# A graph network on one core: addition and residual placed after the next block's weighing, and the projection of q, k and v one block later, ahead of the feed-forward

## The reference

```python
for l in range(2):                                     # layers 0 and 1
    xn = layernorm(h, ln1_g[l], ln1_b[l])
    q, k, v = (xn @ w[l] + b[l] for w, b in (q, k, v))  # 8 heads of 32
    scores = einsum('ehd,ehd->eh', q[dst], k[src]) * scale
    attn = segment_softmax(scores, dst)                # with a self edge per node
    agg = segment_sum(attn * v[src], dst)              # 0 for a node without edges
    h = h + agg @ wo[l] + bo[l]
    xn2 = layernorm(h, ln2_g[l], ln2_b[l])
    h = h + gelu(xn2 @ w1[l] + b1[l]) @ w2[l] + b2[l]
x = x + h
...
mod_k = K[src] + 0.2 * rel_w[edge_type]                # layer 2, 4 heads of 64
out = softmax-weighted sum of V[src]  @ Wo + bo
x = x + layernorm(out + node_features) * gamma + beta
```

## Time and profile before

| | |
|---|---|
| median of 3 runs | 5655.94 us (5652.53 to 5657.53) |
| the profiled execution | 5652.02 us, of it the span 5650.4 us |
| busy: PE, DVE | 3852.2 us (68%), 3863.6 us (68%) |
| busy: POOL, ACT | 3129.7 us (55%), 1896.3 us (34%) |
| DVE waits for `feed_out` (L1252, L1256 on L1570) | 227.2 us in 48 waits, 215.8 us in 48 |
| DVE waits for the exponentials (L1167 on L1361) | 212.3 us in 130 waits |
| DVE waits for the square roots (L578 on L574) | 163.6 us in 192 waits |

### The profile page before, as it was taken

The page is one execution under the profiler, slowest core; times in us unless marked ns, Lnnn a source line. Parts: engine busy times, 40 slices in busy tenths (PEclk is TensorE's granted clock), DMA queues, the critical chain, the costliest instruction groups (busy, mean ns, idle before and its releaser), DMA issues. The chain is left out here.

```text
span 5650.4 us, 101635 instructions
## 1 busy us (share of the span) xinstructions
PE 3852.2 (68%) x17126; PEld 2788.6 (49%) x17127; DVE 3863.6 (68%) x6685; ACT 1896.3 (34%) x4023; POOL 3129.7 (55%) x3068
## 2 busy tenths in 40 slices
PE   2057664688887877746878778777746666666665
PEld 2023332466665665534656656555534455455444
DVE  9633333787776666637877766666469989888876
ACT  5023331233333333322333343333422333333333
POOL 0422224777666655426777655554267777666643
PEclk9987776788888988877989888888866766766666
DMA  4022224676666555436666665554256665555542
GB/s 180 7 62 93 94 94 123 188 216 205 191 184 189 172 166 155 136 106 187 212 213 195 190 192 171 162 162 146 81 145 180 184 178 167 163 163 154 144 131 84
DMA packets 361805, 870.95 MB, mean 154 GB/s; under 512 B 142032, under 2 KB 154813, under 8 KB 361748
## 3 DMA queue, kind: packets, MB, share of 16 engines
q0 software_dynamic: 243088, 718.69, 43.2%
q1 hardware_dynamic: 111604, 119.56, 6.8%
q10 hardware_dynamic: 7056, 32.12, 1.4%
HBM read 791.89 MB, written 149.65 MB: 167 GB/s over the span
## 5 line engine op out<-in xcount | busy, mean ns | idle before, releaser
L1039 POOL DMA_INDIRECT kv<-kv_dram,idx x2616 | 2699.7, 1032 | 1598.8 <-issue 751.2
L1506 PE MATMUL ps_acc<-kv,ident 128*128 x5232 | 1499.1, 457 | 328.9 <-DVE kv L1179 327.7
L1506 PEld LDWEIGHTS ps_acc<-kv,ident 128*128 128x128 f32 x5232 | 1218.6, 236 | 635.2 <-issue 412.1
L1101 DVE TENSOR_TENSOR kv<-kv,ps_q 128x1024 f32 x654 | 785.0, 1213 | 177.1 <-issue 103.7
L1106 DVE TENSOR_REDUCE sc<-kv 128x32 f32 (+2 forms) x654 | 785.5, 1211 | 17.5 <-DVE kv L1101 13.1
L1179 DVE TENSOR_TENSOR kv<-kv,ps_q x654 | 753.6, 1216 | 20.7 <-issue 8.2
L1500 PE MATMUL ps_acc<-acc_scaled,ident 128*128 128x256 f32 x306 | 149.2, 581 | 567.1 <-DVE zrun L1171 567.1
L1557 PE MATMUL ps_big<-xnaT,w_ffn 128*128 128x128 f32 x3136 | 389.4, 284 | 142.5 <-ACT xnaT L1407 142.5
L1557 PEld LDWEIGHTS ps_big<-xnaT,w_ffn 128*128 128x128 f32 x3136 | 372.1, 198 | 164.4 <-ACT xnaT L1407 83.0
L1407 ACT ACTIVATE xnaT<-ps_t,ln 128x128 f32<-128x128 f32 x196 | 79.0, 453 | 1068.5 <-PE ps_t L585 898.7
L1500 PEld LDWEIGHTS ps_acc<-acc_scaled,ident 128*128 128x128 f32 x306 | 61.5, 251 | 620.6 <-DVE zrun L1171 620.6
(11 more groups left out here) (206 smaller groups left out, 5024.8 us busy)
## 6 DMA issues: line engine op xcount, KB each, us to landing
rec_in<-rec_dram SPq DMA_DIRECT2D x147, 512.0 KB, 5.1
rec_dram<-rec_out POOLq DMA_DIRECT2D x98, 512.0 KB, 3.4
kv<-kv_dram,idx POOLq DMA_INDIRECT x2616, 3.7
rec_dram<-rec_in ACTq DMA_DIRECT2D x49, 640.0 KB, 3.0
windows<-kv SPq DMA_DIRECT2D x46, 408.0 KB, 2.6
rec_in<-rec_dram SPq DMA_DIRECT2D x49, 128.0 KB
w_ffn<-in_L_gnn_w SPq DMA_DIRECT2D x4, 1024.0 KB, 6.4
meta<-slot_meta SPq DMA_DIRECT2D x153, 24.0 KB, 2.6
```

The costliest lines, as they stand in the source:

```text
L1039: pool.indirect_dma_start(kv[:, u * W + slot, :], None, kv_dram[l], bass.IndirectOffsetOnAxis(ap=idx[:, u, slot:slot + 1], axis=0), bounds ...
L1101: nc.vector.tensor_tensor(at, at, q, ALU.mult).then_inc(s["mul"], 1)
L1506: mm = nc.tensor.matmul(ps_acc[:, 0:D], ident[:], at[:, :, slot, :].rearrange("p a d -> p (a d)"), start=False, stop=False, skip_group_che ...
```

## The change

Four things are done at once.

1. On DVE `second(b-2)` and `residual(b-1)` stand behind `weigh` of block b, at the end of the iteration. `maxima`, `rescale`, `weight_sums` and `weigh` follow each other without them. This holds in layer 2 too.
2. The scales that go with them are taken one iteration later, right behind `start`: `scales1(b-2)` and `scales2(b-3)`. On ACT the first normalisation stands before the second.
3. q, k and v of the next layer are projected for block b-4 instead of b-3 (`DEPTH` 4), on PE before the feed-forward, and q goes into the second half of the bank of `ps_t`, so that PE waits for ACT's copies of that bank. ACT's `record(b-4)` follows the copy of the first transposes.
4. `feed_out` is cut in two halves, with `project_sums` between them.

```diff
--- before.py
+++ after.py
@@ -46,7 +46,7 @@
 HEADS = [8, 8, 4]
 RING = 4
 SETTLED = []
-DEPTH = 3
+DEPTH = 4
 SCATTER_LAG = 5
 STORE_LAG = 5
 
@@ -207,7 +207,8 @@
         eps_col = sb("eps_col", [P, 1])
 
 
-        ps_t = pb("ps_t", [P, 512])[:, 0:D].rearrange("p (c n) -> p c n", c=KD)
+        ps_t_q = pb("ps_t_q", [P, 512])
+        ps_t = ps_t_q[:, 0:D].rearrange("p (c n) -> p c n", c=KD)
         ps_t2_w = pb("ps_t2_w", [P, 512])
         ps_t2 = ps_t2_w[:, 0:D].rearrange("p (c n) -> p c n", c=KD)
         ps_w = pb("ps_w", [P, 512])
@@ -923,13 +924,13 @@
                 last, chunks_before, earlier, rounds_before = counts
                 return (round_number(rounds_before + earlier), chunks_before + earlier * CPS, last)
 
-            def iterate(eng, iteration, peeled=DEPTH, whole=NB - 1 if typed else NB):
+            def iterate(eng, iteration, peeled=2 if typed else DEPTH, whole=NB - 1 if typed else NB):
 
                 for b in range(peeled):
                     iteration(b)
                 with eng.Fori(peeled, whole) as b:
                     iteration(b)
-                for b in range(whole, NB + DEPTH):
+                for b in range(whole, NB + peeled):
                     iteration(b)
 
             def last_block(b):
@@ -1271,10 +1272,16 @@
                         def second_part():
                             if exists(b - 2):
                                 second(b - 2)
+                        def earlier_scales():
+                            if exists(b - 2):
+                                scales1(b - 2)
+                            if exists(b - 3) and not typed:
+                                scales2(b - 3)
                         if exists(b):
                             counts = blocks.next(b)
                             k, chunk0, filled = last_round(counts)
                             start(b)
+                            earlier_scales()
 
                             def finish_last():
                                 if exists(b - 1):
@@ -1304,23 +1311,17 @@
                                 with dve.If(earlier == 0):
                                     finish_last()
                             scores(b, k, chunk0, filled, finish_late if late else lambda: None)
-                            second_part()
                             maxima(last, k, chunk0, filled)
+                            rescale(last, b, k)
+                            weight_sums(b, k)
+                            weigh(k, chunk0, filled)
                         else:
+                            earlier_scales()
                             if exists(b - 1):
                                 finish(b - 1, dve.snap(blocks.rounds, min_val=1))
-                            second_part()
+                        second_part()
                         if exists(b - 1):
                             residual(b - 1)
-                        if exists(b):
-                            rescale(last, b, k)
-                        if exists(b - 2) and not typed:
-                            scales2(b - 2)
-                        if exists(b - 1):
-                            scales1(b - 1)
-                        if exists(b):
-                            weight_sums(b, k)
-                            weigh(k, chunk0, filled)
 
                     extras = dve.alloc_register(f"l{l}_extras")
                     dve.reg_mov(extras, 0)
@@ -1447,11 +1448,13 @@
                         to = rec_out[:, one(b % OUT_RING), :]
                         act.wait_ge(s["qkv"], b + 1)
                         nc.scalar.copy(flat(to[:, :, 0:2 * D]), ps_kv)
-                        nc.scalar.copy(flat(to[:, :, 2 * D:3 * D]), ps_w[:, 0:D]).then_inc(s["recq"], 1)
+                        nc.scalar.copy(flat(to[:, :, 2 * D:3 * D]), ps_t_q[:, D:2 * D]).then_inc(s["recq"], 1)
 
                     def iteration(b):
                         if exists(b - 2) and not typed:
                             feed_forward(b - 2)
+                        if exists(b - 4) and not typed:
+                            record(b - 4)
                         if exists(b - 3) and not typed:
                             turn_normed(b - 3)
                         if exists(b - 2) and not typed:
@@ -1478,12 +1481,10 @@
                         if exists(b - 1):
                             act.wait_ge(s["var1"], b)
                             deviation(0, s["sd1"])
+                        if exists(b - 1):
+                            normed1(b - 1)
                         if exists(b - 2) and not typed:
                             normed2(b - 2)
-                        if exists(b - 1):
-                            normed1(b - 1)
-                        if exists(b - 3) and not typed:
-                            record(b - 3)
                         if exists(b):
                             free_unused(k, filled)
 
@@ -1559,16 +1560,15 @@
                             if f % 4 == 3:
                                 mm.then_inc(s["f1"], 1)
 
-                    def feed_out(b):
+                    def feed_out(b, half):
                         to = ps_w[:, D:2 * D]
-                        if not isinstance(b, int) or b >= 2:
-                            pe.wait_ge(s["recq"], b - 1)
-                            settle(pe)
-                        bias(to, B_2 + l * D)
-                        for f in range(KF):
+                        if half == 0:
+                            bias(to, B_2 + l * D)
+                        for f in range(half * KF // 2, (half + 1) * KF // 2):
                             pe.wait_ge(s["g"], b * KF + f + 1)
                             mm = nc.tensor.matmul(to, gT[:, f, :], w_2[:, f, :], start=False, stop=(f == KF - 1))
-                        mm.then_inc(s["f2"], 1)
+                        if half == 1:
+                            mm.then_inc(s["f2"], 1)
 
                     def turn_normed(b):
                         pe.wait_ge(s["xn2"], b + 1)
@@ -1582,29 +1582,35 @@
                         project_kv(l + 1, xnbT)
 
                     def next_q(b):
-                        if not isinstance(b, int) or b + 1 < NB:
-                            pe.wait_ge(s["second"], 2 * b + 3)
+                        if not isinstance(b, int) or b + 2 < NB:
+                            pe.wait_ge(s["xTs1"], b + 3)
                             settle(pe)
-                        project_q(ps_w[:, 0:D], l + 1, xnbT).then_inc(s["qkv"], 1)
+                        project_q(ps_t_q[:, D:2 * D], l + 1, xnbT).then_inc(s["qkv"], 1)
 
                     def iteration(b):
                         if exists(b - 2) and not typed:
                             turn_hidden(b - 2)
                         if exists(b - 3) and not typed:
                             turn_normed(b - 3)
+                        if exists(b - 4) and not typed:
+                            next_kv(b - 4)
+                            next_q(b - 4)
                         if exists(b - 2) and not typed:
                             feed_forward(b - 2)
                         if exists(b - 1):
+                            if exists(b - 4) and not typed:
+                                pe.wait_ge(s["recq"], b - 3)
+                                settle(pe)
                             turn_sums(b - 1)
                         if exists(b - 2) and not typed:
-                            feed_out(b - 2)
-                        if exists(b - 3) and not typed:
-                            pe.wait_ge(s["xTs2"], b - 2)
-                            settle(pe)
+                            feed_out(b - 2, 0)
                         if exists(b - 1):
+                            if exists(b - 3) and not typed:
+                                pe.wait_ge(s["xTs2"], b - 2)
+                                settle(pe)
                             project_sums(b - 1)
-                        if exists(b - 3) and not typed:
-                            next_kv(b - 3)
+                        if exists(b - 2) and not typed:
+                            feed_out(b - 2, 1)
                         if exists(b):
                             counts = blocks.next(b)
                             k, chunk0, filled = last_round(counts)
@@ -1616,9 +1622,6 @@
                             earlier_rounds(pe, counts, whole)
                             if typed and not last_block(b):
                                 relation_rows(next_round(k))
-                        if exists(b - 3) and not typed:
-                            next_q(b - 3)
-                        if exists(b):
                             sums(k, chunk0, filled)
 
                     pe.sem_inc(s["used"], 2 * CPS)
```

## The result

| us | before | changed |
|---|---|---|
| median (4 runs each) | 5654.2 (5650.9 to 5657.5) | 5853.1 (5846.1 to 5855.9) |
| ratio | | 1.035, 95% interval 1.0332 to 1.0368 |
| profiled execution, span | 5652.0, 5650.4 | 5851.5, 5849.8 |

The change made the kernel 3.5% slower, 199 us where 118 were forecast. The median, 5853, lies inside the stated range of 5680 to 5905, and 8 us above the case that the prediction called its own (5690 to 5845). A layer's time stands apart in the trace: it is cut at the starts of the maxima's reduction. "Blocks of 6" are the first nine distances, "41 blocks" the rest of a layer, "end" the way to the next layer's first maxima (the last: to the end).

The account below looks back on a forecast made before the run. Below 6 chunks a circle over several engines, not DVE's work, was taken to set the period. 5652.0 - 56 - 39 + 13 + 14 + 172 + 14 = 5770, 5774 for the median, range 5680 to 5905.

Parts of the forecast that it names:

- the case that the prediction called its own: Whole kernel: layers 0 and 1 gain, layer 2 loses more; 5690 to 5845 us, chance 0.60.
- (a): Layers 0 and 1, 4-chunk block: DVE's 5.43 us wait for `feed_out` goes, since `second` comes a whole weighing later.
- (b): Layers 0 and 1: DVE's 0.58 us wait for the square root goes, scales being taken after the next `start`.
- (c): Layers 0 and 1: `residual` leaves the wait for the exponentials; 1.4 us with hand-over is paid behind the weighing.
- (d): Loop's foot and head: DVE's branch and `block_row` loads lie uncovered behind a short statistic, 2.1 us per block (0.76 to 2.6).
- the first rival: DVE's front end runs ahead of the waiting statistics at 147 block ends: 184 us less, 5590, faster; chance 0.12.
- +172 forecast: Layer 2: `second`, `residual` and front end lose their cover; +4.35 us per block of 4 or fewer, +172 in all.
- the circle that remains: Layers 0 and 1, from DVE's first scales to the next over several engines: layer 0 22.8 us plus 1.15 per chunk.
- The clock rival: PE's slow-clock part falls on k, v, q and feed-forward in 52 blocks: +166 us, 5940; chance 0.12.
- the rival's two signs: PE's mean clock in layer 0 falls below 0.89, and the feed-forward matmuls take longer than 3.84 us.
- +14 forecast: Ends of layers 0 and 1: the last two turns each hold a serial k, v, q projection, 2 x 3.5 us per layer.
- The third rival: Layer 2 as forecast, layers 0 and 1 keep today's periods because the circle is longer than counted: 5869 us; chance 0.12.

Follow-up runs that it names:

- e5: The changed kernel with VectorE's two reads of `block_row` moved from the loop's head into the scores: 5598.6 us, 0.990 of the kernel before.
- e12: The kernel before with VectorE's new order in layers 0 and 1 alone and the `block_row` reads in the scores: 5525.9 us, ratio 0.977.
- e3: The changed kernel with the `block_row` reads in the scores, in a job where the kernel before took 7822.7 us: 7567.7 us, ratio 0.968.

## Why the prediction was right, and where its terms were off

**What held.** The sign and its cause. (a) and (b): the waits for f2 went; those for the square roots fell from 83 us to 3 within the layers. (The 164 us of the table before and the 85 of the changed kernel hold 81 and 82 us of the preparation, which the table's words "over the blocks of all layers" leave out.) (c): the exponentials' wait was forecast at 2.4 for 4 chunks and is 2.36 in the block shown; in a block of 4 of layer 1 (the MEMSET at 3520 us) it is 3.69, and over layer 0's 41 blocks 3.2 on average. (d): "issue" idle behind the short statistics, the term against which the first rival stood. That rival decides "if DVE's gap ahead of the start is under about 1 us"; it is 2.3 to 3.6 as a rule, and moving the reads away gave 254 us. The records of the front end show why: the branch starts 0.1 us behind the start of the last statistic, and the reads behind the branch, while under queued weighings both had run ahead.

The prediction held a rule of the Trainium skill against (d), and (d) was no test of it. The Trainium skill, "Perfetto Trace Analysis", section "Per-instruction lifecycle: what the profiler-reported window actually captures", says that on VectorE an instruction with a wait goes into a wait queue and the sequencer fetches the next. The statistics have no wait of their own: each wait is an instruction by itself that the front end runs (L56, at 1721.46 for the last statistic), so neither (d) nor e5 speaks for or against that sentence. Where an instruction waits itself, the trace does not agree with it: in 142 waits of the addition L1168, of 0.3 to 8.4 us, the register instruction behind it started 0.013 to 0.015 us after the addition had started, and not during the wait.

**Where 118 became 199.** Term by term, with what they measured:
- *Layer 2*, +172 forecast, +194: blocks of 4 turned in 33.7 us against 33.0, blocks of 5 in 34.8 against 33.9. The bare front end was 2.34, not 2.1, and with 5 chunks less of the move was taken back than I counted.
- *(d) in layers 0 and 1*, 2.1 forecast: 2.29 as a rule, up to 2.9 in layer 0's blocks of 4 and 3.2 to 3.6 in layer 1's, where the reads took longer. The value was taken near the upper end (2.6) from the earlier trace rows, and that end was still too low for these. The 0.3 that was put in for the branch had no row; the branch and what follows it take 0.3 (1721.66 to 1721.98). It is part of the terms around it, not added to them.
- *Layer 1's blocks of 4*, 28.4 us forecast, 30.4 on average: 36 of the 81 us missing. This is the term that was off most: the circle that remains priced k and v at 1.98, and they ran in 3.78, and the front end at 2.1, where it took 3.2 to 3.6. The clock rival described the first of these, for the 52 blocks of 3 and 4 chunks of both layers, and it came true in 46 of them. But only k, v and q ran slow: the feed-forward behind them took 3.73 us in every block. And layer 0's mean clock rose from 0.88 to 0.90, so neither of the rival's two signs appeared, and its price of 166 us was too high. All blocks of 3 and 4 of these layers missed by about 58 us, with the longer reads in it. That the total still fell into the range is in part luck: a mechanism that had been given 0.12 was at work in most of these blocks, and it cost little.
- *The layers' ends*, +14 forecast, +36. They stay at 121 us in e5 and shrink to 107 and 110 in e12, which has DEPTH 3 and the old place of k, v, q. So these cost 14 and 11 where 7 each was forecast; the other 5 of each end come with VectorE's order and were not looked into.
- *Layer 0's 41 blocks*, -56 forecast, -40: 4-chunk blocks at 28.1 instead of 27.4 and 3-chunk blocks at 27.0 instead of 26.2. The first blocks of 4, whose k and v were fast, took 27.6 to 27.7; later ones, with slow k and v, up to 29.7, and in all blocks of 3 k and v were slow. Against all this *the blocks of 6* cost 8 instead of 27.

The third rival (layers 0 and 1 gain nothing, 5869) is nearest by its sum, 5853, but by its mechanism it is right for layer 1 alone.

## What to carry to other kernels

In this kernel what stands last in a hardware loop should be long: weighings of 1.2 us each hid the loop's branch and register reads, a 0.18 us statistic bared 2.3 us of them per turn, and a 0.42 us addition 2.1. Read what the next turn needs while long instructions run, before judging an order of work. And ask what the engine waits for at the old place. In layers 0 and 1 it waited there for the moved instruction's own input, and the wait went with the move. In layer 2 the instruction stood inside a wait for something else, which stayed and grew, so the move belongs in the first two alone.

## What the runs showed of the hardware

- A register read at the loop's head is dear in this trace: one read of `block_row` took 0.30 us as a rule and up to 1.60. Two reads less at the head, with their checks, brought the "issue" gaps from 2.29 to 0.96 us in layer 0 as a rule, from 2.28 to 1.00 in layer 1 (from about 3.5 in its blocks of 4) and from 2.34 to 0.89 in layer 2. What is left is branch and register work.
- VectorE's front end ran ahead under queued weighings (both reads over 1.0 us before the last weighing ended), and not past a wait.
- TensorE's granted clock: in the block shown it was 1.00 in the sums, and 0.50, the lower of the two levels, in k and v after 4.87 us without work (3.78 us against 1.98). In the block of e5 without a pause it was 1.00. The rest of the trace is less plain: a pause of 1.6 us stood ahead of fast k and v in layer 0 (1755 us) and of slow ones in layer 1 (2870 us), so the pause just before does not decide alone.
- One and the same kernel (e3 and e5) took 7568 and 5599 us. Up to the first maxima it took 961.7 and 962.9, and the layers' ends agree within 14 us; the loops alone are longer. The gelu of e3 (busy, mean ns, idle before):

```profile
L1444 ACT ACTIVATE shared<-ps_big,b 128x128 f32<-128x128 f32 x784 | 221.4, 370 | 1637.7 <-remote 1442.9 <-issue 191.3 <-PE ps_big L1587 3.3
```

and of e5:

```profile
L1444 ACT ACTIVATE shared<-ps_big,b 128x128 f32<-128x128 f32 x784 | 213.8, 383 | 10.3 <-PE ps_big L1587 9.1
```

In one block of e3 (2293 us) ScalarE stood 14.68 us ahead of a gelu whose operands TensorE had finished, for something that the profile only calls remote. In the expectation of e5 I took it for waiting on its own instructions; no row shows that. The queues that carry instructions moved as many packets in both runs (48 and 14), none of them while ScalarE stood. What it was stays open. One chip gave both kinds of job, so it isn't the chip alone.
